# Query projection of the first attention in five passes, with eight on-chip transfers per batch

## What is computed

```
xn = layernorm(x)
Wdkv = xn @ latent_w + latent_b                                  # keys and values, 36 wide
q = einsum('btc,hcl->bhtl', xn, Wd_w) + Wd_b[None, :, None, :]   # queries, 16 heads x 36
scores = einsum('bhtl,bsl->bhts', q, Wdkv) / sqrt(8)
attn = softmax(where(causal, scores, -inf))
y = einsum('bhts,bsl->bhtl', attn, Wdkv)
x = x + transpose(y).reshape(b, t, 16 * 36) @ out_w + out_b + ffn(xn)   # then the second layer
```

## Time and profile before

| | us |
|---|---|
| median of three runs | 1703.63 |
| the profiled execution: time | 1707.66 |
| its span, first to last instruction | 1704.8 |
| first attention, regular steps | about 135 to 759 on the time axis |
| end of the first attention, first feed-forward | 759 to 955 |
| second layer: attention and gate | 955 to 1546 |
| second layer: routed experts | 1546 to 1705 |

### The profile page before, as it was taken

One profiled execution on the slowest core, in us unless ns is written; L12 is line 12 of the kernel. 1 busy time (PEld: TensorE's weight loads), 2 busy tenths in 40 slices (PEclk: granted clock), 3 DMA queues, 4 the chain that ended last, 5 costly groups with the idle time before them and its releaser, 6 DMA issues.

```text
span 1704.8 us, 44671 instructions
## 1 busy us (share of the span) xinstructions
PE 1504.1 (88%) x13893; PEld 1081.1 (63%) x13895; DVE 1131.8 (66%) x2702; ACT 989.5 (58%) x2495; POOL 926.9 (54%) x1633
## 2 busy tenths in 40 slices
PE   7989999999999999997999688888888888885786
PEld 5545555555555555545999577777777777774675
DVE  6566555555555555552555598998898998895662
ACT  6445555555555555542334588888888888872342
POOL 6235555555555545545543566666666666632664
PEclk8789999999999999998999699999999999996775
DMA  9132131222222221213332121211211211215442
GB/s 278 36 83 56 48 78 50 55 54 55 57 57 57 57 57 46 54 52 78 65 70 61 28 49 44 46 41 42 46 43 41 45 43 41 45 38 113 87 91 36
DMA packets 240850, 103.36 MB, mean 61 GB/s; under 512 B 145497, under 2 KB 229274, under 8 KB 240794
## 3 DMA queue, kind: packets, MB, share of 16 engines
q1 hardware_dynamic: 230554, 89.04, 22.4%
q0 software_dynamic: 10240, 13.64, 3.7%
HBM read 57.73 MB, written 35.96 MB: 55 GB/s over the span
## 4 chain that ended last, share of the span: by engine, by line
PE 44%; ACT 15%; DMA 11%; DVE 10%; SPq 9%; issue 7%; POOL 4%; POOLq 0%; DVEq 0%; ACTq 0%
DMA remainders<-yT 5%; PE bankA L1883 4%; PE bankB L1929 4%; PE bankT L1912 4%; PE bankT L2068 4%; SPq L370 4%; DMA dq<-remainders 3%; DVE mneg L998 3%; ACT qx L1688 3%; ACT km L1697 2%; ACT gqx L1688 2%; PE bankT L2187 2%; PE bankS L1897 2%; PE bankA L2169 2%; ACT rows L1761 2%
## 5 line engine op out<-in xcount | busy, mean ns | idle before, releaser
L683 POOL TENSOR_SCALAR_AFFINE_SELECT probs<-probs 128x512 f32<-128x512 f32 x256 | 183.4, 739 | 175.0 <-ACT probs L1574 175.0
L1574 ACT ACTIVATE probs<-bankT 128x1024 f32<-128x1024 f32 x128 | 131.1, 1024 | 194.4 <-PE bankT L1915 194.4
L997 DVE TENSOR_REDUCE mneg<-bankS 128x2 f32<-128x256 f32 x256 | 106.6, 416 | 138.1 <-PE bankS L1902 137.4
L998 DVE TENSOR_REDUCE mneg<-bankS 128x2 f32<-128x512 f32 x256 | 174.3, 681 | 0.0
L1912 PE MATMUL bankT<-qT,kT 37*128 37x512 f32 x512 | 139.4, 623 | 11.4 <-ACT probs L1576 6.5
L676 POOL CAST qb<-qT 128x256 bf16<-128x256 f32 x256 | 96.7, 398 | 86.6 <-ACT qT L1569 86.6
L1929 PE MATMUL bankB<-probs,vaug 128*64 128x512 f32 x512 | 142.5, 636 | 1.0 <-ACT yT L1581 1.0
L1883 PE MATMUL bankA<-xnT,wd 128*128 128x256 f32 x480 | 142.1, 409 | 0.0
L1363 DVE STREAM_TRANSPOSE pt<-pe 128x768 f32<-128x768 f32 x128 | 124.4, 972 | 25.2 <-ACT pe L1674 25.2
L1581 ACT COPY yT<-bankB 128x512 f32<-128x512 f32 x128 | 75.1, 587 | 112.9 <-PE bankB L1933 112.9
L1569 ACT ACTIVATE qT<-bankA,bd 128x256 f32<-128x256 f32 x256 | 107.6, 473 | 55.1 <-PE bankA L1883 55.0
(11 more groups left out here) (319 smaller groups left out, 4286.0 us busy)
## 6 DMA issues: line engine op xcount, KB each, us to landing
rzb<-reciprocals SPq DMA_DIRECT2D x128, 128.0 KB, 2.6
yT<-yT SPq DMA_DIRECT2D x64, 128.0 KB, 2.3
xtab<-tab SPq DMA_DIRECT2D x32, 192.0 KB, 2.0
xs_sorted<-zeros SPq DMA_DIRECT2D x1, 4608.0 KB, 19.4
qT<-xs_sorted SPq DMA_DIRECT2D x144, 32.0 KB, 1.8
ys_sorted<-qT SPq DMA_DIRECT2D x36, 128.0 KB, 1.9
value_rows<-vrow SPq DMA_DIRECT2D x32, 128.0 KB, 1.8
vx<-value_rows SPq DMA_DIRECT2D x256, 16.0 KB, 1.8
```

Of the source, the lines that this page charges most:

```text
L683: pool.affine_select(out=blocks, in_=blocks, compare_op=ALU.is_ge, fill=0.0, base=0, pattern=[[0, 4], [1, P]], channel_multiplier=-1).then ...
L998: dve.tensor_reduce(mneg[:, n.half, :, j, 1], bankS[:, :, 128:384], AX.X, ALU.max, negate=True).then_inc(S["red_done"], 1)
L1574: act.activation(pT[:, g % 2].rearrange("p e j t -> p e (j t)"), bankT[:, 0:2, :], ACT.Exp, scale=SCALE0).then_inc(S["exp_done"], 1)
```

## The change

Ten of the 16 heads are projected as before, in five passes (pairs 0 to 4; FULL is 5). The six heads of pairs 5 to 7 ride along in the unused columns of the first four passes: in each half, 27 of the 36 components of pair 5 + i go to the 27 free columns of pass i, and the 9 that are left of all three pairs fill the 27 free columns of pass 3 (SPLIT is 27, REST is 9). Two copies on VectorE lay the weights out once at the start, and eight more small loads do so for the bias. For each batch SP then issues eight transfers (`moved`: two of 27 rows x 3 KB, six of 9 rows x 1 KB) that bring those rows to their places in qT; they stand between reciprocals_out and reciprocals_in. round_queries of pairs 5 to 7 waits for these transfers on semaphore m_in. On VectorE, invert and normalise 0 each stand one `red` later. The very first batch is projected as before.

```diff
+    FULL = 5
+    SPLIT = 27
+    REST = L - SPLIT
+    MOVES = 2 + 2 * (PAIRS - FULL)
+    def passes_before(n):
+        return 0 if n.opens() else n.b * 3 + 1
+    def queries_before(n):
+        return 0 if n.opens() else n.b * FULL + (PAIRS - FULL)
+    def moved_by(n):
+        return landed_before(n) + (0 if n.opens() else 16 * MOVES)
@@ SP, loads at the start, for e in range(2)
+                bd_m = a["L0_attn_Wd_b"].rearrange("(j e) l -> e l j", e=2)[e]
+                sp.dma_start(bd[LP * e + L + 1:LP * (e + 1), 0:PAIRS - FULL], bd_m[0:SPLIT, FULL:PAIRS]).then_inc(S["w_a"], 16)
+                for i in range(PAIRS - FULL):
+                    o = LP * e + L + 1 + REST * i
+                    sp.dma_start(bd[o:o + REST, 3:4], bd_m[SPLIT:L, FULL + i:FULL + i + 1]).then_inc(S["w_a"], 16)
@@ SP
+            def moved(n):
+                sp.wait_ge(S["q_sb"], queries_before(n) + 4)
+                for e in range(2):
+                    o = LP * e
+                    spare = slice(o + L + 1, o + LP)
+                    sp.dma_start(qT[o:o + SPLIT, n.half, FULL:PAIRS, :], qT[spare, n.half, 0:PAIRS - FULL, :]).then_inc(S[f"m_in{n.half}"], 16)
+                    for i in range(PAIRS - FULL):
+                        r = o + L + 1 + REST * i
+                        sp.dma_start(qT[o + SPLIT:o + L, n.half, FULL + i, :], qT[r:r + REST, n.half, 3, :]).then_inc(S[f"m_in{n.half}"], 16)
-            def denominators(p):
+            def denominators(p, n):
                 denominators_out(p)
                 reciprocals_out(p)
+                if n:
+                    moved(n)
                 reciprocals_in(p)
             maxima(Batch(0, 0))
+            moved(Batch(0, 1))
             maxima(Batch(0, 1))
@@ POOL, round_queries
-                    pool.wait_ge(S["q_sb"], n.b * PAIRS + (j + 1))
+                    if j < FULL or n.opens():
+                        pool.wait_ge(S["q_sb"], queries_before(n) + (j + 1))
+                    else:
+                        pool.wait_ge(S[f"m_in{n.half}"], moved_by(n))
@@ POOL, start
+            pool.memset(qT[:, 1, FULL:PAIRS, :], 0.0)
@@ DVE, step
                     red(n, 0)
+                    red(n, 1)
                 if p:
                     invert(p)
                 if n:
-                    red(n, 1)
                     red(n, 2)
...
                     red(n, 4)
+                    red(n, 5)
                 if p:
                     normalise(p, 0)
                 if n:
-                    red(n, 5)
                     red(n, 6)
@@ DVE, start
+            dve.tensor_copy(wd[:, 0:PAIRS - FULL, :, L + 1:LP], wd[:, FULL:PAIRS, :, 0:SPLIT])
+            dve.tensor_copy(wd[:, 3, :, L + 1:LP].rearrange("p e (i l) -> p e i l", l=REST),
+                            wd[:, FULL:PAIRS, :, SPLIT:L].rearrange("p i e l -> p e i l"))
@@ ACT, qevac
+                    if j >= FULL and not n.opens():
+                        continue
@@ ACT, step
-                    if n and g < GROUPS - 1:
+                    if n and g < 2:
                         qevac(n, g + 1)
@@ PE, step
-                    if n and g < GROUPS - 1:
-                        qproj(n, g + 1, early=early)
+                    if n and g == 1:
+                        qproj(n, 2, (0,), early=early)
```

More of the change, by code:

```diff
@@ L62, in program, with landed_before @@
     GROUPS = PAIRS // 2
+    FULL = 5
[6 more added lines that the diff above has]
+        return 0 if n.opens() else n.b * FULL + (PAIRS - FULL)
+    def landed_before(n):
+        if type(n.pair) is int and n.pair == 0:
+            return 0
+        return n.pair * (16 * (MOVES + 4)) - (16 * MOVES if n.half == 0 else 0)
+    def moved_by(n):
+        return landed_before(n) + (0 if n.opens() else 16 * MOVES)
     ctx = ExitStack()
@@ L315, in passed @@
             eng.sem_inc(S["passed"], 1)
-        NA = 2 * 4 + 4
+        NA = 2 * 4 + 4 + MOVES
         NO = 4 + 2 * (L - LM) + 1
@@ L396, in reciprocals_in @@
                              rec_d.rearrange("e j t -> (e j) t").unsqueeze(1).to_broadcast([H, LX, T])).then_inc(S["zrows_in"], 16)
-            def denominators(p):
+            def denominators(p, n):
                 denominators_out(p)
                 reciprocals_out(p)
+                if n:
+                    moved(n)
                 reciprocals_in(p)
             maxima(Batch(0, 0))
+            moved(Batch(0, 1))
             maxima(Batch(0, 1))
-            denominators(Batch(0, 0))
+            denominators(Batch(0, 0), Batch(1, 0))
             sp.wait_ge(S["zeroed1"], 2)
@@ L426, in _, with pair @@
             sp.dma_start(xtab_d[B * T:B * T + PAD, C:C + E1], zeros[:, 0:E1]).then_inc(S["pads"], 16)
-            def pair(i):
+            def pair(i, last=False):
                 maxima(Batch(i + 1, 0))
-                denominators(Batch(i, 1))
+                denominators(Batch(i, 1), Batch(i + 1, 1))
                 maxima(Batch(i + 1, 1))
-                denominators(Batch(i + 1, 0))
+                denominators(Batch(i + 1, 0), None if last else Batch(i + 2, 0))
             for i in range(3):
@@ L442, in _ @@
             sp.dma_start(b2all[:, :, :], a["L0_ffn_b2"].rearrange("(o e) c -> o e c", o=1).to_broadcast([P, E0, C])).then_inc(S["w_in"], 16)
-            with sp.Fori(3, LOOP) as i:
+            with sp.Fori(3, LOOP - 1) as i:
                 pair(i)
+            pair(LOOP - 1, True)
             def load(i, u):
@@ L655, in fetch_columns @@
             def fetch_columns(m):
-                pool.wait_ge(S["q_ps"], m.b * GROUPS - GROUPS)
+                pool.wait_ge(S["q_ps"], passes_before(m.before()))
                 passed(pool)
@@ L1003, in turn_maxima @@
                 if prior:
-                    dve.wait_ge(S[f"m_in{n.half}"], n.pair * 64)
+                    dve.wait_ge(S[f"m_in{n.half}"], landed_before(n))
                 passed(dve)
@@ L1565, in qevac @@
             def qevac(n, r):
-                act.wait_ge(S["q_ps"], n.b * GROUPS + (r + 1))
+                act.wait_ge(S["q_ps"], passes_before(n) + (r + 1))
                 for k in range(2):
                     j = 2 * r + k
+                    if j >= FULL and not n.opens():
+                        continue
                     act.activation(qT[:, n.half, j, :], bankA[:, k * T:(k + 1) * T], ACT.Identity,
@@ L1880, in qproj @@
                 if 0 in halves and (r or not early or n.half):
-                    pe.wait_ge(S["q_sb"], n.b * PAIRS + 2 * r)
+                    pe.wait_ge(S["q_sb"], queries_before(n) + 2 * r)
                 for k in halves:
@@ L1884, in qproj @@
                                     columns0(n, early), start=True, stop=True)
-                if 1 in halves:
+                if 1 in halves or 2 * r + 1 == FULL:
                     ins.then_inc(S["q_ps"], 1)
@@ L1907, in st @@
                 if g == 0:
-                    pe.wait_ge(S[f"m_in{u}"], b.pair * 64 + 64)
+                    pe.wait_ge(S[f"m_in{u}"], moved_by(b) + 64)
                 if prior:
```

## The result

The changed kernel takes 1756.81 us (median; 1751.75 to 1759.1) against 1705.20 of the kernel before (1703.34 to 1709.86): a ratio of 1.029, 95% interval 1.026 to 1.033. The forecast was 1693, its range 1664 to 1722: wrong in sign and outside the range. The profiled execution has a span of 1754.4 us, 49.6 more than before. A time is the median of a kernel's executions, a ratio compares means with the kernel before on the same chip.

What follows compares the result with a forecast made beforehand. PE was taken to bound the kernel at 22.2 us a step; afterwards SP's circle, 17.7 + 4.0 = 21.7, would. 28 x (21.7 - 22.2) + 3 = -11 us gave 1693 us, range 1664 to 1722.

Steps and rivals of the forecast that it cites:

- What bounds the kernel, and what goes: PE sets the 22.20 us step; without three projections and a bank wait PE alone would need 20.0 us.
- two terms: On PE, per step: three projections fewer save 1.59 us, and the new VectorE order removes a 0.60 us wait.
- The circle on SP: From one issue of the maxima through SP and DVE to the next: 17.7 + M, 21.7 us, the new step.
- M: SP's time for the eight issues between reciprocals_out and reciprocals_in: 4.0 us a step, bounds 3.0 to 5.4.
- fixed part: The circle through SP and DVE without the eight issues: 17.7 us a step.
- the rival of 1718: All eight SP issues cost what the gathers cost: M = 4.9, step 22.6; within the 19% for dearer issues.
- Issue time next to nothing: Rival: SP's eight issues take under 2.3 us, so PE sets the step at 20.0; 1645 us, chance 2%.
- The moves' own way: Moved rows land near 14.9 us into the step; PE waits 1 us ahead of smax 5, at no extra cost.
- PE's clock falls: Rival: 2 us of each step run at PE's lower clock, 1.2 GHz, total 1749 us; chance 4%.
- SP's issues cost more: Rival: from M = 4.5 the circle exceeds 22.2 us and the kernel slows, 1718 or 1732 us; chance 19%.
- The start: Before the regular steps: bias loads 1.5 us and early moves 1.1, together 3 us lost, between 0 and 6.

Runs made afterwards that it cites:

- the issues alone: The kernel before plus the eight transfers at their place, written to a tile nobody reads, with its old passes and VectorE order: 1828.53 us, ratio 1.073.

## Why the prediction was wrong, by its steps

- **What bounds the kernel, and what goes**: right. PE alone needs 19.94 us a step (forecast 20.0), by the runs without moves. Of its two terms the projections gave 1.50 for 1.59 and the order 0.85 for 0.60.
- **The circle on SP**: right as a mechanism. normalise 0 waits for rzr, as the prediction asked for, and the step follows M one for one. Its fixed part came to 17.2 for 17.7: normalise 0 took 0.61 (420.95 to red 6 at 421.56) and normalise 1 0.78 where the earlier trace rows had 0.99 for the same operation; what made it shorter stays open.
- **M: the term that failed.** 6.19 us, forecast 4.0, bounds 3.0 to 5.4: short by 2.2 us a step, or 61 us in 28, all of the difference between -11 and +50; what else was off, the fixed part of the circle (0.5 a step too long) and the clock (0.50, not in the sum), cancels. The bounds were to be the shortest and the longest row of a small transfer, L376 and L362, but 0.63 is the median of L362; its longest issue is 0.817 us, and a bound of 8 x 0.86 = 6.9, with the gap, would have held the measured M. Both rows are also of another kind: L376 goes to DRAM and L362 comes from DRAM; none of the rows read was a transfer within the chip of a number of rows that is not a multiple of 16, and that form, 0.70 to 0.83 in the change, is dearer than the medians of either. "The nearest row" was chosen by size, and size has no price here: the estimate of 0.47 for the six small ones, a mean with the cheap L376, should have been no less than the 0.57 and 0.615 of the transfers within the chip. That gives M = 4.65 to 4.9, a slower kernel and at its upper end the rival of 1718: the right sign, and still too little.
- **Issue time next to nothing**: the Trainium skill ("DMA: Bandwidth & Descriptors", Anatomy of one DMA) puts the sequencer's dispatch at about 50 ns, in a section on DMAs that go by GpSimd's path. The prediction read it as the price of an issue on SP; the issues on SP took 0.33 to 0.84 us in the runs. The same page ("Why a DMA increments its semaphore by 16 and not by 1") says that a transfer is split over the largest number of engines, up to 16, that divides its rows, and that the issuing sequencer writes the rest of the 16 semaphore counts itself. The rows within the chip would agree with a surcharge for that, which the page does not state; the rows to DRAM do not, 9 at 0.33 being cheaper than 16 at 0.51, so the mechanism stays open.
- **The moves' own way**: PE was to wait 1 us ahead of smax 5 and waited 2.39, since the eight moves take 2.2 us longer. By itself the wait costs nothing, as was said: with the clock kept up the step is 23.40 where PE waits for the moves and 23.42 where nobody does. What it does to the clock was the rival.
- **PE's clock falls**: given 4%, against it the second layer's 0.99 at 85% busy. It does fall in this step, and costs 0.50 us (28 x 0.50 = 14 us), not the 2 us of that rival: one round of av loses 0.90 (1.98 for 1.08), and part of that lies beside VectorE's work behind rzr. The Trainium skill's warning ("TensorE: Matmul & The Clock Gate", HAM oscillation) on loops that wait for a DMA in every turn agrees with the trace: 1.98 us for a round of av instead of 1.08. The mean busy share of another stage, put against it, said nothing about a single wait of 2.4 us in every step.
- **The rivals as a set**: SP's issues cost more, and the clock fell; the prediction kept them apart. They go together: a longer M makes PE's wait longer, and the clock fell behind that wait and not where the wait was filled. 28 x (23.40 - 22.29) = 31 of issues, 14 of clock, 3.6 of start and 0.8 behind make the 49.6.
- **The start**: 3.6 for 3, inside 0 to 6, by the first issue of the regular steps.

## What to carry to other kernels

When work leaves the bounding engine and DMAs take its place, count the issues and lay them on the issuing queue's own chain: here each of them took 0.70 to 0.83 us, whether it carried 9 KB or 81. So merge transfers, or issue them where that queue already waits for a landing; the same five passes and the same order were worth -66 us or +52 here, by the number and the place of the issues and what they did to the clock. A price for which the trace has no row of the same kind (direction and row count, not bytes) needs a bound at the longest single issue of the rows at hand, not at a median, and rivals that cause one another get a joint chance and a joint price.

## What the runs showed of the hardware

- SP pays for an issue by its form, not its bytes: within the chip 0.53 to 0.55 us for 16, 32 or 48 rows, 0.64 for 4, 0.67 for 8, 0.70 to 0.84 for 9, 18, 24 and 27 rows; 9 rows to or from DRAM 0.33; 16 rows to DRAM 0.51. 8 rows of 512 bytes from DRAM at the start took 0.63, so this is a table and not yet a rule.
- A wait taken away can cost time: with a wait fewer, PE stopped later in its step, the lower clock fell on work that others waited for, and the kernel took 1797 instead of 1757 us. Matmuls that compute nothing, put into PE's idle time, brought 54 us back there; in the changed kernel they took 0.50 us off the step.
- The work that pays for a wait need not be the next: in the change PE waited 2.39 us, did the scores behind the wait at a granted clock of 0.96, and the round of av after them at 0.50. With the issues alone smax is slow right behind a wait of 2.59 (0.40 for 0.28).
- Two reductions put ahead of the reciprocal and of the first multiply on VectorE were worth 26 us (1.5%) where the multiply's data came in time and 70 (4.2%) where they came late; a share of the clock in the 70 is possible.
